# A mixture-of-experts block on one core: slot regions per expert, the router by halves, four shared units behind each loop

## The chip, the core and the metric

The kernel runs on one core of a Trainium2 chip, in one launch. TensorE (PE), VectorE (DVE), ScalarE (ACT), GpSimd (POOL) and SyncE (SP, which issues the direct DMAs) each run their own instruction stream and meet at semaphores. The metric is the device time of the launch in microseconds. Three runs of the kernel before gave 469.31, 472.06 and 475.77 us; the median is 472.06 us.

## The reference

The input is 1,024 tokens of 256 numbers. Three sublayers follow each other, each with a residual:

```
x = x + 0.5 * ffn(layernorm(x))
x = x + attention(layernorm(x))        # gated linear attention, 2 heads of 128, chunks
x = x + 0.5 * ffn(layernorm(x))        # the same weights as the first ffn

ffn(x):
    shared = (silu(x @ g) * (x @ u)) @ down * sigmoid(x @ sgate)      # width 704
    p = softmax(x @ gate_w.T)                                        # 16 experts
    w, ids = top_k(p, 4)
    for e in range(16):
        coef = sum(where(ids == e, w, 0))
        out += coef * ((silu(x @ w1[e]) * (x @ w3[e])) @ w2[e])       # width 176
    return shared + out
```

Every token goes through the shared expert and through the four experts with its largest probabilities.

## The kernel before, in words

A token tile is 128 tokens, so there are NT = 8. Each ffn (f = 0, 1) has these stages.

- **Norm and router.** DVE normalises the tiles into `XR` (`norm`, L979), PE turns them into `XT` and computes the logits (`logits`, L392). When all 8 are there, DVE picks the four experts of each token (`choose`, L1035), PE ranks the choices by expert (`ranks`, L399), and DVE turns rank plus the expert's first slot into a slot number per choice (`places`, L1066). An expert's slots follow those of the expert before it, rounded up to 128, so `places` needs the counts over all tokens. `tables` (L1084) then computes, for each of the TL = 47 slot tiles, its expert (`tab`) and which rows are real (`valid`).
- **Dispatch.** POOL writes each token's row (normalised values, its 16 coefficients, its number) to its four slots in `slots_dram`: 8 x 4 = 32 indirect DMAs of 128 rows (L881). All slots were filled with zeros at the start (L315, L316; 6.5 MB).
- **Front.** Beside that PE computes the shared expert in 12 units: 6 slices of its width (the last one half as wide) for each half of the tokens. `unit_in` (L406) computes gate and up, ACT the silu, DVE the product (`unit`, L989), `unit_out` (L424) the way back down. FRONT = 11 of the 12 units stand ahead of the slot loop, the last one behind it. ACT and DVE split the experts' weights into a high and a low part between the units (`part` and `part2`, by the tables PARTED and PARTED2); for f = 1 only the low parts are done anew.
- **Slot loop.** 47 tiles: SP loads tile i into one of 6 buffers (L349), PE turns it, multiplies it with the expert's weights, and so on; the expert's number is read from `tab` into a register. POOL adds the result to one of three sum tables in DRAM (L896).
- **Behind the loop.** SP reads the sum tables back (L358, L364), DVE and POOL add them to X (`combine`, `add_tables`), and the shared part of tiles 4 to 7 is added to X once all 12 units are done (L1157). PE then runs 40 warm-up matmuls (L566) and the attention's first turned tiles.

The order of the work is written out by hand in each engine's function. In `attention` PE, ACT and DVE step through the 8 tiles in a loop over i; for f = 1 the norm and the logits of tile t are done inside it (`turned(2, t)`, `logits(1, t)`, `stats(2, t)`, `scale(2, t)`).

## Time and profile before

| | |
|---|---|
| median of 3 runs | 472.06 us |
| the profiled execution | 475.44 us |
| its span | 473.6 us |
| granted TensorE clock, mean | 0.961 |
| PE busy | 420.9 us, 89% |
| DVE busy | 286.2 us, 60% |
| POOL busy | 254.7 us, 54% |
| ACT busy | 210.8 us, 45% |

The profiled execution is 1.8 us longer than its span. A busy share is an average over stages with different limits, so it says little of what a change in one stage is worth. The stages, read off the timeline, in us from the span's start: first norm and router to 31, first front to 92, first slot loop to 193, sums and their way back to 212, attention to 282, second router to 293, second front to 346, second slot loop to 448, end to 473.6.

### The profile page before, as it was taken

The page shows a single profiled execution, that of the slowest core. Times are in us where ns is not written, and L with a number is a line of the kernel's source. Part 1 is how long each engine was busy: PE and PEld are TensorE (multiplying, and loading weights), DVE is VectorE, ACT ScalarE, POOL GpSimd, SP SyncE. Part 2 cuts the span into 40 slices and gives each one's busy share as a digit, 9 for nine tenths or more (in the row PEclk, how much of TensorE's full clock was granted, in tenths as well). Part 3 has the DMA queues.
Part 4 walks back from the last instruction along what each step waited for, and adds up shares of the span by engine and source line. Part 5 has one row for each costly group of instructions (what it writes and reads, how often), then busy time and mean ns, then how long its engine had stood idle before and what let it go on. Part 6 is the DMA issues. An engine that isn't in the chain of part 4 may idle for free.

```text
span 473.6 us, 8663 instructions
## 1 busy us (share of the span) xinstructions
PE 420.9 (89%) x2281; PEld 322.6 (68%) x2281; DVE 286.2 (60%) x843; ACT 210.8 (45%) x580; POOL 254.7 (54%) x209
## 2 busy tenths in 40 slices
PE   5899996799999999879969988999999999999910
PEld 3646553588999998534549964555668999999710
DVE  6485746666666666226496648675456666666406
ACT  2314537556666666303745641111125666666500
POOL 6037773047777777555055201776707677777710
PEclk9999999899999999897998999999999999999965
DMA  7999997369998776770000039722257788777665
GB/s 261 409 357 388 244 365 273 125 144 191 195 173 137 128 135 90 142 237 34 1 1 0 2 122 379 287 72 96 96 185 117 129 138 133 134 133 126 70 172 204
DMA packets 50477, 78.39 MB, mean 166 GB/s; under 512 B 5664, under 2 KB 41504, under 8 KB 49568
## 3 DMA queue, kind: packets, MB, share of 16 engines
q1 hardware_dynamic: 33824, 56.47, 36.3%
q0 software_dynamic: 16608, 21.37, 28.1%
q8 instruction: 22, 0.36, 0.3%
q14 instruction: 23, 0.19, 0.1%
HBM read 41.69 MB, written 36.13 MB: 164 GB/s over the span
## 4 chain that ended last, share of the span: by engine, by line
PE 57%; DMA 11%; DVE 10%; POOL 9%; issue 7%; ACT 4%; SPq 0%; DVEq 0%; POOLq 0%; another core or an unknown queue 0%; ACTq 0%
POOL slots L881 7%; DMA sums<-ar,idx 6%; PE ps L468 6%; PE ps L464 5%; PE ps L465 5%; PE ps L449 4%; PE ps L437 4%; PE ps L476 3%; PE ps L551 3%; PE ps L415 3%; PE ps L420 3%; PE ps L494 2%; PE ps L389 2%; PE ps L382 2%; PE ps L496 2%
## 5 line engine op out<-in xcount | busy, mean ns | idle before, releaser
L896 POOL DMA_INDIRECT sums<-ar,idx x94 | 145.4, 1547 | 85.2 <-ACT ar L735 73.6
L881 POOL DMA_INDIRECT slots<-XR,pos x64 | 72.3, 1130 | 65.1 <-DVE pos L1082 43.0
L1108 DVE SCALAR_TENSOR_TENSOR ar<-ps,XR,ar 128x176 f32<-128x176 f32 x94 | 37.6, 400 | 63.6 <-ACT ar L720 58.9
L464 PE MATMUL ps<-WH,xt 128*128 x188 | 62.2, 332 | 1.9 <-ACT xt L715 1.9
L465 PE MATMUL ps<-WL,xt 128*128 x188 | 60.7, 323 | 0.0
L720 ACT ACTIVATE ar<-ps 128x176 f32<-128x176 f32 x94 | 29.8, 317 | 64.4 <-PE ps L468 51.8
L437 PE MATMUL ps<-WS,ar 128*128 128x256 f32 (+1 forms) x192 | 48.3, 397 | 10.5 <-DVE ar L995 6.3
L437 PEld LDWEIGHTS ps<-WS,ar 128*128 128x128 f32 (+1 forms) x192 | 37.0, 197 | 28.3 <-issue 16.7
L709 ACT ACTIVATE ar<-ps 128x512 f32<-128x512 f32 (+1 forms) x24 | 14.3, 595 | 80.6 <-PE ps L415 65.1
L415 PE MATMUL ps<-XT,WS 128*128 128x512 f32 x96 | 47.4, 617 | 0.0
L468 PE MATMUL ps<-WH,xl 128*128 x188 | 46.5, 328 | 0.5 <-DVE xl L1125 0.3
L1125 DVE TENSOR_TENSOR xl<-ps,xt 128x256 fp32r<-128x256 f32 x94 | 39.8, 424 | 8.4 <-issue 4.4
L735 ACT ACTIVATE ar<-ps 128x256 f32<-128x256 f32 x94 | 36.1, 384 | 17.0 <-PE ps L500 13.3
L715 ACT ACTIVATE xt<-ps 128x256 fp32r<-128x256 f32 x94 | 36.1, 384 | 12.0 <-PE ps L449 11.7
L1119 DVE TENSOR_TENSOR hl<-ps,ht 128x256 fp32r<-128x256 f32 x94 | 39.2, 417 | 1.4 <-ACT ht L725 1.4
L449 PE MATMUL ps<-cst,XR 128*128 128x128 f32 x188 | 37.4, 280 | 0.6 <-DMA XR<-slots 0.2
L420 PE MATMUL ps<-XT,WS 128*128 128x512 f32 x80 | 37.7, 593 | 0.0
L464 PEld LDWEIGHTS ps<-WH,xt 128*128 128x128 f32 x188 | 35.2, 187 | 3.2 <-issue 2.8
L476 PE MATMUL ps<-cst,ar 128*128 128x128 f32 x188 | 36.0, 273 | 0.9 <-DVE ar L1113 0.5
L725 ACT ACTIVATE ht<-ps 128x256 fp32r<-128x256 f32 x94 | 35.7, 380 | 1.0 <-PE ps L476 1.0
L995 DVE TENSOR_TENSOR ar<-ps,ar 128x512 f32<-128x512 f32 x20 | 13.8, 690 | 36.7 <-PE ps L420 16.2
L465 PEld LDWEIGHTS ps<-WL,xt 128*128 128x128 f32 x188 | 35.4, 188 | 0.1
(155 smaller groups left out, 835.7 us busy)
## 6 DMA issues: line engine op xcount, KB each, us to landing
XR<-slots SPq DMA_DIRECT2D x94, 138.0 KB
WR<-w SPq DMA_DIRECT2D x8, 1408.0 KB, 13.9
slots<-ar SPq DMA_DIRECT2D x1, 6072.0 KB, 22.4
W2R<-w2a SPq DMA_DIRECT2D x2, 2048.0 KB
WR<-sums SPq DMA_DIRECT2D x16, 256.0 KB, 5.2
sums<-zeros SPq DMA_DIRECT2D x20, 128.0 KB
sums<-ar SPq DMA_DIRECT2D x2, 1152.0 KB
sums<-X SPq DMA_DIRECT2D x2, 1024.0 KB, 5.1
```

What stands on the lines that cost most here:

```text
L415: mm = pe.matmul(ps[:, 4 + u % 2, :], WS1[:, k, 2 * j, :], XT[:, k, half(h)], start=k == 0, stop=k == KD - 1)
L420: mm = pe.matmul(ps[:, 6 + u % 2, :], WS1[:, k, 2 * j + 1, :], XT[:, k, half(h)], start=k == 0, stop=k == KD - 1)
L437: mm = pe.matmul(ps[:, 2 * h + i // 2, i % 2 * D:(i % 2 + 1) * D], Hs[u % 2][rows, tok(i)], WS2[rows, j, :], start=first and i % 2 == 0, s ...
L449: mm = pe.transpose(ps[:, i % 2, k * P:(k + 1) * P], xs[i % NX][:, k * P:(k + 1) * P], ident)
L464: pe.matmul(to, token, WH[:, bass.ds(e, 1), k, :].rearrange("p a n -> p (a n)"), start=k == 0, stop=False)
L465: pe.matmul(to, token, WL[:, bass.ds(e, 1), k, :].rearrange("p a n -> p (a n)"), start=False, stop=False)
L468: mm = pe.matmul(to, xl[i % 2][:, k * P:(k + 1) * P], WH[:, bass.ds(e, 1), k, :].rearrange("p a n -> p (a n)"), start=False, stop=k == KD - 1)
L476: mm = pe.transpose(ps[:, 6 + i % 2, c * P:(c + 1) * P], hm[i % 2][:, c * P:(c + 1) * P], ident)
L881: pool.indirect_dma_start(out=slots_dram[:, :], out_offset=bass.IndirectOffsetOnAxis(ap=pos[:, t, r:r + 1], axis=0), in_=XR[:, t, :], in_o ...
L896: pool.indirect_dma_start(out=sums_dram[f][a][:, :], out_offset=bass.IndirectOffsetOnAxis(ap=idx[:, i:i + 1], axis=0), in_=ys[i % NY], in_ ...
L1119: dve.tensor_tensor(hl[i % 2], ps[:, 6 + i % 2, 0:2 * P], ht[i % 2].bitcast(F32), ALU.subtract).then_inc(s_hl, 1)
L1125: dve.tensor_tensor(xl[i % 2], ps[:, i % 2, 0:D], xt[i % 2].bitcast(F32), ALU.subtract).then_inc(s_xl, 1)
```

## The change

Every expert gets a region of CAP = 1,152 rows of `slots_dram`, at a fixed start. A slot number is now the rank plus a constant, so it needs no counts of the later tokens. The router (`choose`, `ranks`, `places`, ACT's `router`) runs by halves of four tiles, and POOL's dispatch waits for one half at a time. For f = 0 half 0 is routed before the second half is normalised; for f = 1 it is routed inside the attention's loop, and half 1 behind it. The fill at the start shrinks to one tile; instead SP writes one tile of zeros behind the last token of each expert (16 DMAs, `tails`), at an address that it reads into a register. `counts` and `tables` also compute the first row of each slot tile, and SP reads it into a register before each of the 94 loads. FRONT goes from 11 to 8, so four units stand behind each loop; the tables PARTED and PARTED2 move with it. POOL signals by a memset behind its last add, and SP waits for that before it reads the sums back.

```diff
-PARTED = {3: (0, 3), 4: (3, 6), 5: (6, 9), 6: (9, 13), 7: (13, NE)}
+PARTED = {1: (0, 2), 2: (2, 6), 3: (6, 10), 4: (10, 14), 5: (14, NE)}
-PARTED2 = {8: (0, 8), 9: (8, NE)}
+PARTED2 = {5: (0, 4), 6: (4, 12), 7: (12, NE)}
-SLOTS = TL * P
+CAP = N + P
+SLOTS = NE * CAP + P
-FRONT = UNITS - 1
+FRONT = (8, 8)
+HT = NT // 2
...
-            fill = slots_dram.rearrange("(p t) n -> p (t n)", p=P)
-            most = TL // ZR * ZR * ROW
-            sp.dma_start(fill[:, 0:most].rearrange("p (t n) -> p t n", n=ZR * ROW), spread(blank, 1, TL // ZR)).then_inc(s_fill, 16)
-            sp.dma_start(fill[:, most:], blank[:, 0:TL % ZR * ROW]).then_inc(s_fill, 16)
+            sp.dma_start(slots_dram[NE * CAP:, :], zeros[:, :]).then_inc(s_fill, 16)
...
+            def row(of, i):
+                return nc.values_load(of[0:1, i:i + 1], engines=[mybir.EngineType.SP], min_val=0, max_val=NE * CAP,
...
+            def tails(f):
+                sp.wait_ge(s_last, f + 1)
+                for e in range(NE):
+                    sp.dma_start(slots_dram[bass.ds(row(last_row, e), P), :], zeros[:, :]).then_inc(s_fill, 16)
+            tails(0)
...
+                    tails(1)
+                sp.wait_ge(s_tab, f + 1)
+                sp.wait_ge(s_fill, 16 * (1 + NE * (f + 1)))
                 sp.wait_ge(s_disp, 16 * NT * TOPK * (f + 1))
                 for i in range(TL):
                     wait(sp, s_hm, TL * f + i - NX + 1)
-                    sp.dma_start(xs[i % NX], slots_dram[tok(i), :]).then_inc(s_xs[i % NX], 16)
+                    sp.dma_start(xs[i % NX], slots_dram[bass.ds(row(first_row, i), P), :]).then_inc(s_xs[i % NX], 16)
...
+                sp.wait_ge(s_added, f + 1)
...
+            def ranks(f, h):
+                pe.wait_ge(s_sel, 2 * f + h + 1)
+                if h == 1:
+                    count = ps[:, 3, RK + NT * NE:RK + NT * NE + NE]
+                    pe.matmul(count, ones[:, :], upto[0][:, :, HT - 1], start=True, stop=False)
+                    pe.matmul(count, ones[:, :], upto[1][:, :, HT - 1], start=False, stop=True)
+                to = ps[:, ranks_bank(f, h), RK + h * HT * NE:RK + (h + 1) * HT * NE]
+                pe.matmul(to, ones[:, :], upto[h][:, :, :].rearrange("p e t -> p t e"), start=True, stop=False)
+                if h == 1:
+                    pe.matmul(to, ones[:, :], spread(upto[0][:, :, HT - 1], 1, HT), start=False, stop=False)
+                pe.matmul(to, minus_later, gt[:, tiles_of(h), :].rearrange("p t e -> p (t e)"), start=False, stop=True).then_inc(s_rank, 1)
...
                 if u == NJ:
-                    pe.wait_ge(s_pos, f + 1)
-                if u == FRONT:
+                    pe.wait_ge(s_tab, f + 1)
+                if u == FRONT[f]:
...
-                    for t in range(NT + 1):
-                        if t < NT:
+                    for t in range(HT + 1):
+                        if t < HT:
                             turned(0, t)
                         if t > 0:
                             logits(0, t - 1)
-                unit_in(f, 0)
-                ranks(f)
-                unit_in(f, 1)
-                unit_out(f, 0)
-                for u in range(2, FRONT):
+                    unit_in(0, 0)
+                    ranks(0, 0)
+                    unit_in(0, 1)
+                    for t in range(HT, NT + 1):
+                        if t < NT:
+                            turned(0, t)
+                        if t > HT:
+                            logits(0, t - 1)
+                    unit_out(0, 0)
+                    unit_in(0, 2)
+                    ranks(0, 1)
+                else:
+                    pe.wait_ge(s_pos, 3)
+                    unit_in(1, 0)
+                    ranks(1, 1)
+                    pe.wait_ge(s_sgx, 4)
+                    unit_in(1, 1)
+                    unit_out(1, 0)
+                    unit_in(1, 2)
+                unit_out(f, 1)
+                for u in range(3, FRONT[f]):
...
+                    if i == NT + 3:
+                        ranks(1, 0)
...
+                    if c == 0 and 2 * q == HT:
+                        router(0, 0)
...
                     norm(0)
-                router(f)
-                for u in range(FRONT):
+                    unit(0, 0)
+                router(f, 1)
+                for u in range(1 - f, FRONT[f]):
                     unit(f, u)
                     if f == 0:
                         part(u)
                         part2(u)
                 slots(f)
-                for u in range(FRONT, UNITS):
+                for u in range(FRONT[f], UNITS):
...
+                    if i == NT + 1:
+                        router(1, 0)
...
-                pool.wait_ge(s_fill, 32)
-                pool.wait_ge(s_pos, f + 1)
                 for t in range(NT):
+                    pool.wait_ge(s_pos, 2 * f + t // HT + 1)
...
+                pool.memset(mark[:, :], 0.0).then_inc(s_added, 1)
...
+            def choose(f, h):
+                some = tiles_of(h)
+                dve.wait_ge(s_lg, 2 * f + h + 1)
...
+            def places(f, h):
+                some = tiles_of(h)
+                dve.wait_ge(s_rank, 2 * f + h + 1)
+                rank = ps[:, ranks_bank(f, h), RK + h * HT * NE:RK + (h + 1) * HT * NE].rearrange("p (t e) -> p t e", e=NE)
+                link(dve.tensor_tensor(lg[:, some, :], rank, spread(base1, 1, HT), ALU.add))
+                link(dve.tensor_tensor(ex[:, some, :], lg[:, some, :], gt[:, some, :], ALU.mult))
+                for t in range(HT * h, HT * (h + 1)):
+                    ins = dve.max(m8[:, t, :], ex[:, t, :])
+                link(ins)
+                dve.tensor_scalar(pos[:, some, :], m8[:, some, 0:TOPK], -1.0, None, ALU.add).then_inc(s_pos, 1)
+            def counts(f):
+                dve.wait_ge(s_rank, 2 * f + 2)
+                count = ps[:, 3, RK + NT * NE:RK + NT * NE + NE]
+                dve.scalar_tensor_tensor(last_row[:, :], count, -1.0, base1, ALU.add, ALU.add).then_inc(s_last, 1)
                 link(dve.tensor_scalar(ti[:, :], count, float(P - 1), None, ALU.add))
                 link(dve.tensor_scalar(ti[:, :], ti[:, :], 7, None, ALU.logical_shift_right))
                 link(dve.tensor_copy(tf[:, :], ti[:, :]))
                 link(dve.tensor_tensor_scan(cum[:, :], ones[:, 0:NE], tf[:, :], 0.0, ALU.mult, ALU.add))
                 link(dve.tensor_tensor(low[:, :], cum[:, :], tf[:, :], ALU.subtract))
                 link(dve.tensor_scalar(low[:, :], low[:, :], float(P), None, ALU.mult))
...
                 dve.tensor_tensor(high[:, :], low[:, :], count, ALU.add)
-                dve.tensor_scalar(pos[:, :, :], m8[:, :, 0:TOPK], -1.0, None, ALU.add).then_inc(s_pos, 1)
+                link(dve.tensor_scalar(tf[:, :], tf[:, :], float(-P), float(CAP), ALU.mult, ALU.add))
...
+                link(dve.tensor_tensor(cmp[:, :, :], cmp[:, :, :], spread(tf[:, :], 1, TL), ALU.mult))
+                link(dve.tensor_reduce(v2[:, :], cmp[:, :, :], AX.X, ALU.add))
+                link(dve.scalar_tensor_tensor(v2[:, :], tile_no, float(P), v2[:, :], ALU.mult, ALU.add))
+                dve.tensor_scalar(first_row[:, :], v2[:, :], float(NE * CAP), None, ALU.min)
...
             def ffn(f):
-                choose(f)
-                places(f)
-                unit(f, 0)
-                unit(f, 1)
+                if f == 0:
+                    unit(0, 0)
+                    choose(0, 1)
+                    unit(0, 1)
+                    places(0, 1)
+                else:
+                    choose(1, 1)
+                    places(1, 1)
+                    unit(1, 0)
+                    unit(1, 1)
+                counts(f)
                 tables(f)
-                for u in range(2, NJ + 1):
-                    unit(f, u)
-                    part(f, u)
-                shared_sums(f, 0, NJ)
-                for u in range(NJ + 1, FRONT):
+                part(f, 1)
+                for u in range(2, FRONT[f]):
                     unit(f, u)
                     part(f, u)
                     part2(f, u)
-                shared_sums(f, 1, FRONT)
+                    if u == NJ:
+                        shared_sums(f, 0, NJ)
+                shared_sums(f, 1, FRONT[f])
                 slots(f)
-                for u in range(FRONT, UNITS):
-                    unit(f, u)
+                if f == 0:
+                    for u in range(FRONT[f], UNITS):
+                        unit(f, u)
...
+                    if i == NT + 1:
+                        choose(1, 0)
+                    if i == NT + 2:
+                        places(1, 0)
...
-            norm(0, lambda t: None)
...
+            norm(0, range(HT), lambda t: None)
...
+            choose(0, 0)
+            places(0, 0)
+            norm(0, range(HT, NT), lambda t: None)
             ffn(0)
-            norm(1, lambda t: combine(0, t))
+            norm(1, range(NT), lambda t: combine(0, t))
             attention()
             ffn(1)
             for t in range(NT):
+                if t < 2:
+                    unit(1, FRONT[1] + 2 * t)
+                    unit(1, FRONT[1] + 2 * t + 1)
                 combine(1, t)
```

Three places where instructions move, in the words of the built programs. First, DVE in the first norm. Before, the last two tiles are scaled and the whole router follows:

```order
L971 BN_STATS st<-X 128x6 [waits s_x3]
L972 BN_AGGR mv<-st 128x2 [waits s_chain]
L977 TENSOR_SCALAR XR<-X,mv,rstd 128x256 [waits s_mv,s_rs] x2
L1179 COPY XR<-ics 128x8 [waits s_ics]
L1038 TENSOR_REDUCE t<-ps 128x8 [waits s_lg,s_cst]
L1039 TENSOR_TENSOR lg<-ps,t 128x128 [waits s_chain]
L1041 TENSOR_REDUCE t<-ex 128x8 [waits s_ex]
L1042 RECIPROCAL t<-t 128x8 [waits s_chain]
```

In the changed kernel the same four statistics stand behind the first half's slot numbers (`pos`), and the first unit's product (L1065) stands ahead of the second half's `choose`:

```order
L1146 TENSOR_SCALAR pos<-m 128x16 [waits s_chain]
L1041 BN_STATS st<-X 128x6 [waits s_x2]
L1042 BN_AGGR mv<-st 128x2 [waits s_chain]
L1041 BN_STATS st<-X 128x6 [waits s_x2]
L1042 BN_AGGR mv<-st 128x2 [waits s_chain]
L1041 BN_STATS st<-X 128x6 [waits s_x3]
L1042 BN_AGGR mv<-st 128x2 [waits s_chain]
L1047 TENSOR_SCALAR XR<-X,mv,rstd 128x256 [waits s_mv,s_rs] x2
L1041 BN_STATS st<-X 128x6 [waits s_x3]
L1042 BN_AGGR mv<-st 128x2 [waits s_chain]
L1047 TENSOR_SCALAR XR<-X,mv,rstd 128x256 [waits s_mv,s_rs] x2
L1065 TENSOR_TENSOR ar<-ps,ar 128x512 [waits s_uu,s_usi]
```

So `choose` and `places` of half 0 moved ahead of the statistics of tiles 4 to 7, and the product of unit 0 ahead of `choose` of half 1.

Second, DVE at the end of the attention. Before, the last token tiles are added to X (L1236), their statistics taken and scaled, and the router (L1038) follows:

```order
L1236 SCALAR_TENSOR_TENSOR X<-ps,rr,X 128x256 [waits f_r]
L971 BN_STATS st<-X 128x6 [waits s_xu]
L972 BN_AGGR mv<-st 128x2 [waits s_chain]
L977 TENSOR_SCALAR XR<-X,mv,rstd 128x256 [waits s_mv,s_rs]
L1236 SCALAR_TENSOR_TENSOR X<-ps,rr,X 128x256 [waits f_r]
L971 BN_STATS st<-X 128x6 [waits s_xu]
L972 BN_AGGR mv<-st 128x2 [waits s_chain]
L977 TENSOR_SCALAR XR<-X,mv,rstd 128x256 [waits s_mv,s_rs] x2
L1038 TENSOR_REDUCE t<-ps 128x8 [waits s_lg]
```

In the changed kernel `choose` of half 0 stands ahead of the last of these adds (L1327), and its `places` (L1141 to L1146) ahead of the last scale. The rows begin with the last two of `choose`:

```order
L1134 TENSOR_SCALAR t<-sgt 128x4 [waits s_sgx]
L1135 RECIPROCAL gate<-t 128x4 [waits s_chain]
L1327 SCALAR_TENSOR_TENSOR X<-ps,rr,X 128x256 [waits f_r,s_chain]
L1041 BN_STATS st<-X 128x6 [waits s_xu]
L1042 BN_AGGR mv<-st 128x2 [waits s_chain]
L1047 TENSOR_SCALAR XR<-X,mv,rstd 128x256 [waits s_mv,s_rs]
L1141 TENSOR_TENSOR lg<-ps,cst 128x64 [waits s_rank]
L1142 TENSOR_TENSOR ex<-lg,gt 128x64 [waits s_chain]
L1144 MAX m<-ex 128x8 [waits s_chain]
L1144 MAX m<-ex 128x8 x3
L1146 TENSOR_SCALAR pos<-m 128x16 [waits s_chain]
L1047 TENSOR_SCALAR XR<-X,mv,rstd 128x256 [waits s_mv,s_rs]
```

The last tile's add, statistics and scale now stand behind the whole of `choose`, and the scale behind `places` too.

Third, PE behind the first slot loop: the units, the 40 warm-up matmuls and the first turned tile. Before:

```order
L498 MATMUL ps<-W2H,hl 128x256 [waits s_hl]
L500 MATMUL ps<-W2B,hl 128x256
L415 MATMUL ps<-XT,WS 128x512 [waits s_uh]
L415 MATMUL ps<-XT,WS 128x512
L437 MATMUL ps<-WS,ar 128x256 [waits s_uh,s_y]
L437 MATMUL ps<-WS,ar 128x256 x3
L382 MATMUL ps<-warm 128x512 x40
L389 MATMUL ps<-cst,XR 128x128 [waits s_xc,s_xn]
```

In the changed kernel three more units stand there; the rows show the last part of them:

```order
L459 MATMUL ps<-XT,WS 128x512
L464 MATMUL ps<-XT,WS 128x512 x2
L481 MATMUL ps<-WS,ar 128x256 [waits s_uh]
L481 MATMUL ps<-WS,ar 128x256 x3
L459 MATMUL ps<-XT,WS 128x512 [waits s_uh]
L459 MATMUL ps<-XT,WS 128x512
L481 MATMUL ps<-WS,ar 128x256 [waits s_uh]
L481 MATMUL ps<-WS,ar 128x256 x3
L481 MATMUL ps<-WS,ar 128x256 [waits s_uh]
L481 MATMUL ps<-WS,ar 128x256 x3
L419 MATMUL ps<-warm 128x512 x40
L426 MATMUL ps<-cst,XR 128x128 [waits s_xc,s_xn]
```

The 40 warm-up matmuls and the turned tile behind them stand behind all four units.

## Rows read from the trace of the kernel before

**Rows 1.** Page, the chain that ended last, shares by line.
```profile
POOL slots L881 7%; DMA sums<-ar,idx 6%; PE ps L468 6%; PE ps L464 5%; PE ps L465 5%; PE ps L449 4%; PE ps L437 4%; PE ps L476 3%; PE ps L551 3%; PE ps L415 3%; PE ps L420 3%; PE ps L494 2%; PE ps L389 2%; PE ps L382 2%; PE ps L496 2%
```

**Rows 2.** Table by window, first slot loop: busy time by engine, clock, DMA.
```profile
92.00:194.00 102.00, 99.91 (x707) 91.72 (x706) 64.73 (x236) 60.86 (x187) 69.68 (x45) 1.00 0.80 150
```

**Rows 3.** Chain of waits, first front: start us, us, what.
```profile
32.78 1.72 PE ps L415 x4
...
36.21 1.73 PE ps L437 x8
```

**Rows 4.** Timeline, end of the first front: start us, us, engine, line.
```profile
42.07 2.48 DVE L1007 TENSOR_TENSOR WL<-WR,WH 128x704 fp32r<-128x704 f32 x3
...
69.94 0.60 ACT L709 ACTIVATE ar<-ps 128x512 f32<-128x512 f32 x1 [4.50 <-PE ps L415]
...
85.46 3.57 PE L437 MATMUL ps<-WS,ar 128*128 128x256 f32 x8 [4.28 <-DVE ar L995]
...
91.96 0.36 DVE L1125 TENSOR_TENSOR xl<-ps,xt 128x256 fp32r<-128x256 f32 x1
```

**Rows 5.** Timeline, both dispatches on POOL, and SP behind them.
```profile
30.98 1.14 POOL L881 DMA_INDIRECT slots<-XR,pos  x1 [23.18 <-DVE pos L1082]
...
74.99 1.13 POOL L881 DMA_INDIRECT slots<-XR,pos  x1 [0.30 <-issue]
...
80.77 2.71 SPq L349 DMA_DIRECT2D XR<-slots  x6
...
293.10 1.03 POOL L881 DMA_INDIRECT slots<-XR,pos  x1 [19.84 <-DVE pos L1082]
...
340.37 1.96 POOL L881 DMA_INDIRECT slots<-XR,pos  x1 [0.30 <-issue]
...
343.83 2.71 SPq L349 DMA_DIRECT2D XR<-slots  x6
```

**Rows 6.** Timeline, PE behind the first slot loop.
```profile
193.40 1.88 PE L415 MATMUL ps<-XT,WS 128*128 128x512 f32 x4
...
199.35 9.76 PE L382 MATMUL ps<-warm 128*128 128x512 bf16 x40
212.10 1.42 PE L389 MATMUL ps<-cst,XR 128*128 128x128 f32 x4 [2.99 <-DVE XR L977]
```

**Rows 7.** Timeline, end of attention and second router: PE, then DVE.
```profile
277.03 0.52 PE L395 MATMUL ps<-WG,XT 128*128 128x17 f32 x4
...
278.03 0.48 DVE L1236 SCALAR_TENSOR_TENSOR X<-ps,rr,X 128x256 f32<-128x256 f32 x1 [1.71 <-ACT rr L836]
...
282.63 0.29 DVE L1038 TENSOR_REDUCE t<-ps 128x8 f32<-128x128 f32 x1 [2.42 <-PE ps L395]
...
288.43 0.20 DVE L1064 RECIPROCAL gate<-t 128x8 f32<-128x8 f32 x1
...
290.62 0.29 DVE L1076 TENSOR_TENSOR lg<-ps,low 128x128 f32<-128x128 f32 x1
...
293.48 0.18 DVE L1090 COPY idx<-ics 128x47 int32<-128x47 int32 x1
...
299.64 0.21 DVE L1095 TENSOR_TENSOR valid<-v 128x47 int32<-128x47 f32 x1
```

**Rows 8.** Timeline, behind the second slot loop: PE, then DVE.
```profile
447.93 1.88 PE L415 MATMUL ps<-XT,WS 128*128 128x512 f32 x4
...
461.93 1.68 DVE L1152 TENSOR_TENSOR X<-X,WR 128x256 f32<-128x256 f32 x4 [10.77 <-DMA WR<-sums]
...
471.01 0.48 DVE L1026 SCALAR_TENSOR_TENSOR X<-ps,gate,X 128x256 f32<-128x256 f32 x1
```

**Rows 9.** Chain of waits, a table load of ACT and what follows.
```profile
233.87 1.28 ACT L799
235.17 0.64 ACT ar L803
```

**Rows 10.** Chain of waits, a register read of DVE.
```profile
94.20 0.52 DVEq L1099
```

147 lines of the change are left out of this document (74 added, 73 removed).

## The prediction

> **What bounds the kernel now.** I read the page first: no engine bounds the whole, and the dispatch has the largest single share of the chain of waits, 7% [rows 1]. So the time is a sum of stages, and I read each from the timeline.
>
> In the first slot loop PE is busy 99.9 of 102 us at full clock [rows 2]. The change alters nothing in that loop but SP's loads, so the loops (2.17 us a tile, 47 tiles, twice) are kept. What counts is when each loop starts and what follows it.
>
> - First front: the first dispatch goes out at 30.98 and the last at 74.99, SP loads the first slot tile at 80.77 [rows 5], but DVE begins the loop at 91.96 [rows 4]. The dispatch is not the limit there: ACT and DVE are still splitting weights, and PE waits 4.28 us for them [rows 4].
> - Second front: dispatch from 293.10, last one at 340.37, slot load at 343.83 [rows 5]. Here the dispatch is the limit, since the weights' high parts are already there.
> - Behind the first loop: PE ends the loop at 193.40, has one half unit and 40 warm-up matmuls, waits 2.99 us and turns the first tile at 212.10 [rows 6]. The sums' way through DRAM is the limit, by 3 us only.
> - Behind the second loop: from 447.93 to DVE's last add at 471.01 (ends 471.49); DVE waited 10.77 us for the sums until 461.93 [rows 8].
>
> **Prices.** On PE one unit is `gate`, `up` and `out`, 1.72 us each by the chain's spacing: 1.72 (L415) and 1.73 (L437) [rows 3], the L420 group as L415. That is 5.16 us, and 3.45 for a half-wide unit. A whole `choose` on DVE lasts from 282.63 to 288.63, 6.0 us, `places` from 290.62 to about 292.3, 1.7 us, `tables` from 293.48 to 299.85, 6.4 us [rows 7]. With half the width these are chains of short dependent operations, so they do not halve: I take 4.6 and 1.2 us (bounds: half and whole, 3.0 to 6.0 and 0.8 to 1.7). A low part of one expert is 0.83 us (2.48 for three) [rows 4].
>
> **Term 1, the first front.** The times here are estimates, walked operation by operation with the prices above. Half 0 has its slot numbers at about 21.7: its four logits are ready at about 13.5, `choose` takes 4.1 until its scan, PE is inside unit 0 until about 19.3, then ranks and `places`. POOL starts at 22.3 rather than 30.98. Its 32 DMAs take 45 us as before, since half 1's slot numbers come at 39.5, long before POOL has done 16. The slot loads could start at 22.3 + 45.1 + 4.7 (from the last DMA's end to the load, before) = 72.
>
> DVE and ACT are later. The second half's statistics now follow `places` on DVE, unit 0 ends at about 31.5, `choose` and `places` of half 1 at 39.5. ACT loads its table for silu, for exp, and for silu again, two loads more than before. A load takes 1.28 us and the next operation starts 0.02 us after it [rows 9], so I price them at 2.6 us, half of it hidden while DVE ends its product: 1.3 us, in the 39.5. Then `counts` (new, nine short operations, 1.9 us), `tables` with two more passes of 0.94 and two short ones (8.7 us), low parts of two experts (1.7 us): unit 2's product on DVE ends at 52.4. PE has had only one more `unit_in` in the meantime and stands from 43.4 to 52.4. From there PE paces units 3 to 5: silu of unit 5 at 61, and 1 us later because after 9 us without work it starts at the lower clock, as the 8 matmuls behind the 4.28 us wait show (3.57 us instead of 1.73) [rows 4]. From silu of the third last unit before the loop to the loop itself it was 91.96 - 69.94 = 22.0 us [rows 4]. The same work follows silu 5, with two more high parts (1.4 us) and 1 us of waits for DVE between them: 62 + 24.4 = 86.4. The gain is 91.96 - 86.4 = **5.5 us**. Bounds: 14 us if only the dispatch limited it, -1 us if PE's wait spreads.
>
> The 6.5 MB fill that is gone and the 2.2 MB of tails cost nothing here: the tails' addresses are ready at 40, 16 of them at 0.97 us (0.52 us for a register read [rows 10] and 0.45 for an issue, 2.71 us for six [rows 5]) end at 56, far before 72. If a tail took 2.0 us they would still end at 72.
>
> On the table load: the trace has 1.31 us from its start to the next operation. The Trainium skill (ScalarE: Activation LUTs, What ACT_TABLE_LOAD costs) states about 2.66 us for a switch, a drain of 1.38 us included. By that the two loads would cost 2.8 us more and term 1 would be about 3 us; the trace decides, and it shows no drain.
>
> **Term 2, behind the first loop.** PE has units 8 to 11: 3 x 5.16 + 3.45 = 18.9 us, then 40 warm-up matmuls, 9.76 before [rows 6], 8.7 at full clock. The first tile is turned 27.7 us behind the loop's end instead of 212.10 - 193.40 = 18.7: 9.0 us later. The 3 us limit by the sums is gone, nothing else takes its place: DVE's product of unit 11 ends 17 us behind the loop, its statistics follow by 19. Some comes back, since PE no longer waits ahead of the turned tiles: the first two took 1.42 us for four matmuls [rows 6], twice what they take at full clock, and 8 warm-up matmuls behind them ran as slowly; at full clock the ten-odd matmuls save 1.7 us. I take **+7.3 us**. Bounds: +5 (DVE and ACT also catch up) and +10.
>
> **Term 3, end of attention and second front.** The logits of tile 3 end at 277.5, DVE's add of tile 7 started at 278.03 [rows 7]. Now `choose` of half 0 stands between: 277.6 to 282.2, so that add, and with it the last tile, the weights' reload and half 1's logits, are 4.2 us later. `places` of half 0 adds 1.3 to the last scale. Half 0's slot numbers come at 285.0, POOL starts at 285.9 instead of 293.10: **7.2 us earlier**. Half 1's come at 294, before POOL has done 16 DMAs at 306. Dispatch takes 50.7 us from its first DMA to the slot load, as before [rows 5], so the load is at 336.6, and 0.5 us later for the register read before it [rows 10]. PE has 8 units from 287: 38 us, a stand of 4 us at `tables`, then 18 warm-up matmuls: about 336.5. DVE ends its last sums at 336.2. Dispatch, PE and DVE meet within 1 us. I take **-6.7 us** (bounds -8 and -2, the second if PE or DVE is late by 5).
>
> **Term 4, the end.** PE's four units end 19.1 us behind the loop. DVE waits for the sums until 14.0 us behind it, as before (461.93) [rows 8], then it has two products of about 0.7 us between the adds, and unit 11's cannot end before 17.1. From there 3 tiles of 0.84 (1.68 for two) and 4 of 1.38 (0.48 more for the shared part, and a gap) end at 25.2 us [rows 8]; before it was 471.49 - 447.93 = 23.6. **+1.6 us** (bounds +0.5 and +4). POOL's memset and SP's wait for it delay the first readback by 1.7 us; it hides beside the last add's landing, and costs at most those 1.7.
>
> **Sum.** -5.5 + 7.3 - 6.7 + 1.6 = -3.3 us. The profiled execution of before took 475.44 us, so its like would take 472.1. That execution is among the slowest of the runs shown, 3.4 us above the median; taken from the median, 472.06 - 3.3 = **468.8 us**.
>
> **Rivals.**
>
> *The units behind the loops are free and the first front comes down to its dispatch.* For it: DVE waits 10.77 us behind the second loop [rows 8], and the dispatch would allow a load at 72. Against it: the 40 warm-up matmuls stay behind the units on PE. Price: term 1 up to -14, term 2 at +5, term 3 at -7, term 4 at +1: -15, or 457 us; with the bounds only half reached, -11. About 459 us. Chance 0.22.
>
> *SP's register reads slow the slot loop; this ends slower.* The place is SP's queue in the loop: each load now waits for a read of `first_row`, and the next read starts only when the load is issued. With 0.45 us for the issue and 2.17 us a tile it decides from a read of 1.7 us, in the first loop's 19 tiles with a zeroing DMA from 1.3. At 2.2 us it would cost 0.48 x 94 + 0.43 x 19 = 53 us, 522 us. Against it: DVE reads such a register in every tile, 0.52 us at the longest seen [rows 10]. The Trainium skill (DMA: Bandwidth & Descriptors, Latency and other measured facts) has a floor of about 600 ns for such a read, which would not decide either. Chance 0.05.
>
> *The halves buy nothing*: term 1 is eaten by PE's and DVE's stands, and the second dispatch grows because the weights' reload (7.6 MB) and the tails now run beside it. The second dispatch took 49.2 us for 32 DMAs [rows 5], 1.54 each; at 1.7 the second front gains 1.6 us only. Sum 0 + 7.3 - 1.6 + 1.6 = +7: 479 us. Chance 0.13, a third of it above 2%.
>
> **How the numbers follow.** The forecast has 0.60, within 461 to 477. From the rivals the range takes the first down to 458 and leaves the other tails out: 458 to 478. Two per cent, about what a measurement can tell from no change here, is 9.4 us: faster means below 462.6. The first rival lies mostly there (0.18), and the forecast's low end adds 0.04; slower is the second rival, a third of the third and a little of the forecast, 0.10. Same: 0.68.
>
> **What would show it.** First POOL dispatch near 22 and 286; DVE's first `xl` of the loop near 86; PE idle some 9 us while DVE runs `tables` in the first front; the first turned tile 28 us behind the first loop; SP's slot loads at their old spacing; DVE's last add 25 us behind the second loop. The forecast is wrong if PE does not stand in the first front, or if the loop takes more than 2.2 us a tile.

## The result, and the profile after

The changed kernel took 483.06 us (median of 4 runs, 481.72 to 483.61), the kernel before 471.14 us beside it (469.31 to 475.77). The ratio is 1.023, with a 95% interval of 1.015 to 1.031. I had forecast 468.8 us, 458 to 478: both the direction and the range were wrong.

The profiled executions are 482.55 us after and 475.44 us before, so the profiles have 7.1 us of the difference. Both are cut at the same points. "Left" is VectorE's first `xl` of a slot loop, "keys" the first matmul of `keys_in`.

| stretch, us | before | after | my term | measured |
|---|---|---|---|---|
| start to first left | 91.96 | 91.15 | -5.5 | -0.8 |
| first loop | 101.4 | 103.1 | 0 | +1.7 |
| loop to keys | 24.95 | 31.25 | +7.3 | +6.3 |
| keys to second left | 128.5 | 127.5 | -6.7 | -1.1 |
| second loop | 101.0 | 100.7 | 0 | -0.3 |
| end | 23.6 | 24.9 | +1.6 | +1.3 |

Both losses are about as large as I had said. The two gains are missing. The changed kernel's page shows that the dispatch, 7% of the chain before [rows 1], has left it, and that 2% are waits whose end it puts down to "another core or an unknown queue" ("remote" in the other views):

```profile
PE 76%; DVE 12%; ACT 5%; issue 4%; another core or an unknown queue 2%; DMA 1%; DVEq 0%; ACTq 0%
```

**First front.** This is the timeline around the second half's ranks (start, duration, engine, line, and in brackets the idle time before and what ended it):

```profile
33.94 0.69 DVE L1065 TENSOR_TENSOR ar<-ps,ar 128x512 f32<-128x512 f32 x1
...
37.94 0.35 PE L448 MATMUL ps<-gt,cst 128*128 128x64 f32 x2
...
40.96 0.96 POOL L949 DMA_INDIRECT slots<-XR,pos  x1 [0.30 <-issue]
41.62 1.88 PE L464 MATMUL ps<-XT,WS 128*128 128x512 f32 x4
44.48 0.23 DVE L1141 TENSOR_TENSOR lg<-ps,cst 128x64 f32<-128x64 f32 x1 [9.85 <-remote]
44.63 0.60 ACT L775 ACTIVATE ar<-ps 128x512 f32<-128x512 f32 x1 [5.78 <-remote]
...
45.89 0.96 POOL L949 DMA_INDIRECT slots<-XR,pos  x1 [3.97 <-DVE pos L1146]
```

The first store is early as forecast (21.74, before 30.98 [rows 5]). But VectorE, which waits for the ranks of L448, does not go on at 38.3, when they end. It goes on at 44.48, 9.85 us idle, and ScalarE's wait for TensorE ends 0.15 us later. The releaser is "remote": the view finds no instruction that ended just before. The event itself is in the trace, among the recorded semaphore updates. TensorE's update for the ranks stands there at 44.46, and its next three, for matmuls that end at 40.07, 41.78 and 43.50 by the timeline, at 44.55, 44.61 and 44.67. So it is TensorE's updates that are late, in a bunch; VectorE and ScalarE go on 0.02 us behind theirs. `places`, the counts and the tables all come 6 us later than the matmuls would allow, and VectorE then works with few gaps to 91.15.

The profile of the kernel before has such late updates too, in its first front, and I had overlooked them: ScalarE waits there for a `gate` that ends at 58.97 and whose update is recorded at 62.78. In e19 below, the same program up to its warm-ups ahead of the loop, each update of TensorE's in that stretch comes within 0.02 us. The first row is of before, the second of e19:

```profile
62.81 0.60 ACT L709 ACTIVATE ar<-ps 128x512 f32<-128x512 f32 x1 [5.25 <-remote]
```
```profile
59.02 0.60 ACT L709 ACTIVATE ar<-ps 128x512 f32<-128x512 f32 x1 [2.24 <-PE ps L415]
```

Its first left comes at 87.18, with 18 warm-ups more ahead of it, against 91.96. So the 91.96 that I took for the front of before holds some 5 us of these late updates, and the -0.8 is measured from there.

**Behind the first loop.** TensorE (compare [rows 6]):

```profile
194.25 1.88 PE L459 MATMUL ps<-XT,WS 128*128 128x512 f32 x4
...
213.47 8.81 PE L419 MATMUL ps<-warm 128*128 128x512 bf16 x40
222.11 0.60 PE L426 MATMUL ps<-cst,XR 128*128 128x128 f32 x4
...
225.50 1.10 PE L613 MATMUL ps<-XT,WR 128*128 128x512 f32 x2 [0.62 <-ACT XT L750]
```

The first turned tile is 27.9 us behind the loop; I had 27.7. No idle time stands before it: the 40 warm-ups do, while VectorE had the tile ready at about 213.5.

**Second front.** TensorE, then GpSimd, SyncE and VectorE (compare [rows 5, 7]):

```profile
296.33 1.44 PE L419 MATMUL ps<-warm 128*128 128x512 bf16 x3
...
297.56 3.37 PE L459 MATMUL ps<-XT,WS 128*128 128x512 f32 x4
```
```profile
292.62 1.03 POOL L949 DMA_INDIRECT slots<-XR,pos  x1 [12.22 <-DVE pos L1146]
...
313.69 0.97 POOL L949 DMA_INDIRECT slots<-XR,pos  x1 [5.99 <-DMA slots<-XR,pos]
```
```profile
346.48 4.46 SPq L385 DMA_DIRECT2D XR<-slots  x6
348.21 4.05 PE L419 MATMUL ps<-warm 128*128 128x512 bf16 x18
...
352.99 0.42 DVE L1209 TENSOR_TENSOR xl<-ps,xt 128x256 fp32r<-128x256 f32 x1 [1.17 <-issue]
```

The attention was 7.1 us later, so the first store at 292.62 is, counted from `keys_in`, 7.6 us earlier, as forecast (7.2). From it to the slot load 53.9 us pass, not 50.7. TensorE leaves the attention at the lower clock (granted 0.50 from 292 to 300; three warm-ups 1.44 us, four `gate` matmuls 3.37 instead of 1.88), ends its units at 348.2, and has 18 warm-ups left before it may turn the first slot tile.

### The profile page after: what moved, and what is told of

Same layout as the page of the kernel before. It is cut to its first block, busy times and chain, and to the rows that moved or that the text cites. A ratio compares the mean times of both kernels' runs of the same rounds, so it can differ in the third digit from the quotient of the medians.

```text
span 480.7 us, 9177 instructions
## 1 busy us (share of the span) xinstructions
PE 427.9 (89%) x2297; PEld 328.8 (68%) x2297; DVE 295.6 (61%) x895; ACT 214.2 (45%) x586; POOL 252.0 (52%) x211
## 4 chain that ended last, share of the span: by engine, by line
PE 76%; DVE 12%; ACT 5%; issue 4%; another core or an unknown queue 2%; DMA 1%; DVEq 0%; ACTq 0%
PE ps L459 8%; PE ps L512 7%; PE ps L481 7%; PE ps L508 7%; PE ps L509 6%; PE ps L464 6%; PE ps L493 5%; PE ps L520 4%; PE ps L419 4%; PE ps L613 3%; PE ps L538 3%; PE ps L540 2%; PE ps L539 2%; PE ps L542 2%; PE ps L544 2%
## 5 line engine op out<-in xcount | busy, mean ns | idle before, releaser
L949 POOL DMA_INDIRECT slots<-XR,pos x64 | 69.4, 1085 | 56.1 <-DVE pos L1146 30.1
L481 PE MATMUL ps<-WS,ar 128*128 128x256 f32 (+1 forms) x192 | 51.3, 416 | 22.3 <-DVE ar L1065 15.1
L481 PEld LDWEIGHTS ps<-WS,ar 128*128 128x128 f32 (+1 forms) x192 | 38.8, 207 | 38.7 <-issue 16.7
L786 ACT ACTIVATE ar<-ps 128x176 f32<-128x176 f32 x94 | 29.9, 318 | 67.2 <-PE ps L512 38.3
L459 PE MATMUL ps<-XT,WS 128*128 128x512 f32 x96 | 50.1, 648 | 0.0
L464 PE MATMUL ps<-XT,WS 128*128 128x512 f32 x80 | 37.6, 592 | 0.0
L512 PEld LDWEIGHTS ps<-WH,xl 128*128 128x128 f32 x188 | 31.2, 191 | 5.3 <-DVE xl L1209 4.4
```

The source lines that it names most:

```text
L459: mm = pe.matmul(ps[:, 4 + u % 2, :], WS1[:, k, 2 * j, :], XT[:, k, half(h)], start=k == 0, stop=k == KD - 1)
L464: mm = pe.matmul(ps[:, 6 + u % 2, :], WS1[:, k, 2 * j + 1, :], XT[:, k, half(h)], start=k == 0, stop=k == KD - 1)
L481: mm = pe.matmul(ps[:, 2 * h + i // 2, i % 2 * D:(i % 2 + 1) * D], Hs[u % 2][rows, tok(i)], WS2[rows, j, :], start=first and i % 2 == 0, s ...
L512: mm = pe.matmul(to, xl[i % 2][:, k * P:(k + 1) * P], WH[:, bass.ds(e, 1), k, :].rearrange("p a n -> p (a n)"), start=False, stop=k == KD - 1)
L949: pool.indirect_dma_start(out=slots_dram[:, :], out_offset=bass.IndirectOffsetOnAxis(ap=pos[:, t, r:r + 1], axis=0), in_=XR[:, t, :], in_o ...
```

## The experiments

Every kernel ran beside the kernel before on the same chip; ratios are to that, with 95% intervals. The stretches are from each one's profile, cut as above.

**One half of the change each.** e1 has the halves and regions, with eleven units ahead of each loop:

```diff
-FRONT = (8, 8)
+FRONT = (11, 11)
```

> The changed kernel with eleven units ahead of each loop again (and the splitting of the weights spread as before): regions and halves alone. Theory (the four units behind each loop cost 6.3 and 1.3 us there and each front is bound by TensorE and VectorE, no longer by the dispatches): three more units of 5.7 us lengthen each front by about 17 us, the stretches behind the loops fall by 7.6, so 483 + 34 - 7.6, about 509 us; first slot's subtraction near 108 us. Rival (units are free in a front that waits for dispatches): 483 - 7.6 = 475 us, first slot's subtraction near 91.

Measured: 499.1 us, ratio 1.052 [1.044, 1.061]; first left 104.2, loop to keys 23.0, keys to second left 142.6. So the units are not free ahead of the loops: three of them cost 13.0 and 15.1 us there, and what moving them gives back is 8.2 us behind the first loop and 3.9 at the end. The direction of the first theory holds, its size was 10 us too large.

e2 is the kernel before with `FRONT = 8` and the change's `PARTED` tables.

> The kernel before with only the units moved: eight ahead of each loop, four behind. Theory: the first front falls from 91.96 to the end of its dispatches and the slot load after them (80.77 plus 2 to 3, so 83 to 84), the second stays at its dispatches (0), behind the loops +6.3 and +1.3: 471 - 8.5 + 7.6, about 470 us. Rival (the front is held by splitting the weights on VectorE, which the units covered): 471 + 7.6 = 479 us with the first slot's subtraction still past 90.

Measured: 480.8 us, 1.013 [1.004, 1.022], 11 us above the first theory. First left 84.9 (-7.1), loop to keys 31.24 (+6.3) and end +1.3 are as expected within 1.5. But the second front was 5.0 longer, which no theory had, and the loops 1.8 and 1.1. Part of the 5.0 is the clock: the warm-ups between the last tiles of the attention ran at the lower one (granted 0.50 from 280 to 286), and the logits came 2.9 us later behind the last sum than before. TensorE:

```profile
280.01 1.44 PE L382 MATMUL ps<-warm 128*128 128x512 bf16 x3
...
351.63 0.69 PE L449 MATMUL ps<-cst,XR 128*128 128x128 f32 x2 [16.19 <-DMA XR<-slots]
```

The second line is TensorE's wait for the first slot tile: 16.2 us, so with eight units a second front of whole stores is bound by its stores. No update of TensorE's that ended a wait is late in it.

**Term 2: the warm-ups.**

```diff
-                keep_warm(40, 4)
+                keep_warm(4, 4)
```

> The changed kernel with 4 instead of 40 warm-up matmuls between the units behind the first loop and the attention's first turned tile. Theory (the four units took the place of the warm-ups, and both now stand in a row ahead of that tile): the tile comes 5 to 8 us sooner, 475 to 478 us in all. Rival (the tile waits for the adds of the sums or VectorE's norms anyway): the same 483 us, TensorE idle in place of the warm-ups; or the clock falls without them and the projections lose what is won.

Measured: 476.1 us, 1.009 [1.005, 1.013]. Loop to keys falls from 31.25 to 24.1, less than the 24.95 of before. TensorE:

```profile
213.72 1.04 PE L419 MATMUL ps<-warm 128*128 128x512 bf16 x4
214.59 0.60 PE L426 MATMUL ps<-cst,XR 128*128 128x128 f32 x4
```

So term 2 was these warm-ups, which the units had made needless.

**Term 1: what VectorE waits for.** e4 loads half of `WR`, `W2Q` and `W2R` only behind the counts:

```diff
             for e in range(0, NE, 4):
+                if e == 8:
+                    sp.wait_ge(s_last, 1)
```

> The changed kernel with the last half of the experts' first weights and all of their second weights loaded only once the counts of the first router are there (about 41 to 46 us). Theory (VectorE's 9.85 us ahead of the second half's places are an instruction fetch that stands behind weight loads in full DMA queues): that wait falls to the 4.3 us in which TensorE's ranks come, the counts and tables 5 us sooner, 478 us in all. Rival (it is the dispatches' traffic, or something apart from the loads): the wait stays at 9 us or more, and 483 us.

Measured: 484.3 us, 1.021 [1.014, 1.028], VectorE's wait 9.88 us. The table by window (busy of PE, PEld, DVE, ACT, POOL; clock; DMA share; GB/s), of the changed kernel and of e4, shows that the queues were much less busy in e4 (DMA share 0.34 against 0.96):

```profile
35.00:40.00 5.00, 5.00 (x25) 3.60 (x24) 0.00 (x0) 3.31 (x5) 3.78 (x5) 1.00 0.96 197
```
```profile
35.00:40.00 5.00, 5.00 (x23) 3.41 (x23) 0.00 (x0) 3.31 (x5) 3.78 (x5) 1.00 0.34 113
```

My first explanation, full queues of weight loads, is refuted. e5 holds the stores in its place:

```diff
-                    pool.wait_ge(s_pos, 2 * f + t // HT + 1)
+                    pool.wait_ge(s_pos, 2 * f + (t // HT + 1 if f == 1 else 2))
```

> The changed kernel with the first front's stores to the slots held until both halves have their places (about 39 to 46 us) in place of starting at 21.7. Theory A (the stores' traffic or GpSimd's work is what keeps VectorE and ScalarE waiting to 44.5 us): the wait ahead of the second half's places falls from 9.9 to the 4 us in which TensorE's ranks come, places near 39. Theory B (something in VectorE's own instruction stream at that point): the wait stays at 9.9. Either way the stores then run to about 39 + 41 = 80 (A) or 46 + 41 = 87 us (B), and the first slot is held to 84 to 91; 480 to 485 us.

VectorE, and at the end the same engine at the loop:

```profile
39.39 0.23 DVE L1141 TENSOR_TENSOR lg<-ps,cst 128x64 f32<-128x64 f32 x1 [4.16 <-PE ps L448]
...
93.38 0.42 DVE L1209 TENSOR_TENSOR xl<-ps,xt 128x256 fp32r<-128x256 f32 x1 [7.33 <-ACT xt L781]
```

The wait is 4.16 us and ends with the ranks: theory A, and e6, e7 and e8 on the same chip have it at 9.8 to 9.9. Its second front, where the stores run as in the changed kernel, still has late updates (1.45 and 4.6 us). Without the 7.33 us for late stores VectorE would have been ready at 86.0; I had forecast 86.4. The time is 484.2 us, 1.024 [1.016, 1.033], since the stores now end at 87.8.

e6 puts 64 one-column memsets ahead of VectorE's first norm.

> The changed kernel with 64 memsets of one column ahead of VectorE's first norm (0 to 2 us of work), so that each later instruction of VectorE stands 64 places further in its stream. Theory B (VectorE waits at a place of its instruction stream, such as the edge of a fetched block): the 9.9 us wait ahead of the second half's places moves to another instruction or goes, ScalarE's of 5.8 us stays; if it lands where VectorE waits anyway, 478 us. Rival (the wait belongs to the data: ranks, stores): it stays at that line with 9 to 10 us, and 483 to 485 us.

Measured: 482.8 us, 1.023 [1.014, 1.032]; the wait stayed at its line with 9.87 us. It is not a place in VectorE's instruction stream. The Trainium skill (Runtime: NRT & Kernel Launch, Instruction fetch mechanics) has fetched blocks of 256 instructions, of which one more 16 KB block is read while the last is executed. The changed kernel's page agrees on the size (queue q8, instruction: 22 packets, 0.36 MB). An edge of such a block would have moved by 64. That TensorE's own stream is at fault, whose updates are the late ones, was not tested.

e9 issues 8 stores early and the rest behind the second half's places; e17, the same with 12:

```diff
-                    pool.wait_ge(s_pos, 2 * f + t // HT + 1)
+                    pool.wait_ge(s_pos, 2 * f + (1 if t < 2 else 2))
```

> The changed kernel with a pause in the stores: the first 8 go out as soon as the first half has its places, the other 24 once the second half has. In the first front 8 stores are issued by 32 us, 2 us before VectorE begins to wait for TensorE's ranks. Theory (stores in flight hold that wait to 22.7 us after the first of them): the wait falls to 4.2 us, places near 39.4, first slot's subtraction at 86 to 87 as the prediction had it; in the second front 1 to 2 us more: 476 us. Rival (any early store starts the same 22.7 us): wait stays 9.9, 483 us.

> The changed kernel with the pause behind 12 early stores instead of 8, so that stores are issued until 37 us, across the begin of VectorE's wait at 34.6. Theory (the wait lasts while stores issued ahead of it are under way, and ends with them): it ends 2 to 3 us after the last of the 12, at 39 to 40 us, 1 us past the ranks. Rival (a fixed 22.7 us after the first store): 44.5 us as in the changed kernel.

e9: 481.0 us, 1.012 [1.005, 1.018]; VectorE:

```profile
39.25 0.23 DVE L1141 TENSOR_TENSOR lg<-ps,cst 128x64 f32<-128x64 f32 x1 [4.05 <-PE ps L448]
...
85.78 0.36 DVE L1209 TENSOR_TENSOR xl<-ps,xt 128x256 fp32r<-128x256 f32 x1
```

e17: 475.4 us, 1.008 [1.003, 1.013]; wait 3.58 us, first left 85.6. The first front is now as long as forecast (86.4). Of the 5.4 us that it gains on the changed kernel e9 keeps only 2 in the median: its second front is 1.9 longer than the changed kernel's and its second loop 2.2, where TensorE stood 4.48 us for the first slot tile. e17's second front is 1.9 shorter. A wait of fixed length behind the first store (22.7 us in the changed kernel) is not seen in either.

e12 waits for each of the first 16 stores before the next.

> The changed kernel with each of the first half's 16 stores waited for by GpSimd before it issues the next (in the first front), so that at most one is in flight while VectorE waits for the ranks. Theory C (the number in flight holds the wait): it falls to 4.2 us. Theory D (GpSimd's issuing of stores alone does): it stays 6 us or more beyond the ranks. The first half's stores end later (16 of 3 to 4 us, to 70 to 85 us), so the first front is then bound by them: 485 to 495 us, and only the wait is read.

Measured: 511.7 us, 1.079 [1.070, 1.087]; the wait is 3.77 us and ends with the ranks, although stores were under way. That would be theory C, but its second front, in which nothing was changed, has lost its late updates as well.

Another rival stands beside e9, e12 and e17, and no run tests it: the chip. e1 to e4 ran on one, e5 to e8 on a second, and there each kernel with halves has late updates in one front or both. e9 to e19 ran on three others, and in none of their ten profiles does a late one end a wait, in either front. The changed kernel itself has no profile there. So only e5, among its like on the same chip, shows that holding the stores ends the wait in the first front; that a pause or spacing does is not shown.

**Term 3: the second front.** e7 moves `tables` behind unit 3, e8 has `keep_warm(6, B_KV)` instead of 3 a step and 8 ahead of the first unit.

> The changed kernel with the 10 us of tables on VectorE moved behind the unit with number 3, in both fronts. Theory (in the first front VectorE is busy from 44.5 to 91 us and its sum stays, in the second TensorE stands 5.0 us for it and is then at the lower clock): first slot's subtraction unchanged in the first front (within 1 us), 4 to 6 us sooner in the second, 478 us. Rival (TensorE's stand is only moved behind the tables): the same 483 us.

> The changed kernel with more warm-up matmuls at the attention's end (6 instead of 3 a step and 8 ahead of the second front's first unit). Theory (TensorE comes out of the attention at the lower clock: the unit's first four matmuls take 3.37 us instead of 1.88): they take 1.9 us, the ranks of the second half come 1.5 to 3 us sooner, 480 to 481 us. Rival (the chain waits for ScalarE and VectorE there, or the extra matmuls delay logits): 483 us or above.

e7: 482.9 us, 1.022 [1.014, 1.030]; first left 90.6, second front 128.2. The rival holds. In the first front TensorE's stand of 14.6 us became two, of 6.1 and 4.8; in the second its stand of 5.0 us was only moved (5.98, up to 332.55), and nothing was gained. e8: 483.0 us, 1.024 [1.015, 1.032]. The four `gate` matmuls take 1.88 us, as the theory had it, and the ranks' matmuls end 1.2 us sooner (302.5). But their update came at 305.2, 2.7 us late; VectorE's wait grew from 4.29 to 5.71 us and ended at 305.3, in the changed kernel at 305.4.

Then I added up what had worked. e10 is e9 with 4 warm-ups behind the first loop, e11 also has 4 instead of 18 ahead of the second loop.

> The kernel of the stores with a pause, and 4 warm-ups in place of 40 behind the first loop. The two savings lie in different stretches and should add: 483 - 5 to 7 - 7, 469 to 471 us, no slower than the kernel before. Rival: the pause saves nothing, 476 us.

> As the one with the pause and 4 warm-ups behind the first loop, and 4 in place of 18 ahead of the second loop, where TensorE's units now end at 348 and the slot load is issued at 346.5: those 18 (4.05 us) no longer stand in the shadow of the stores. Theory: 2 to 3 us less, 466 to 468 us. Rival (the first slot load has not landed sooner, or the loop starts at the lower clock): no difference to that kernel.

e10: 474.7 us, 1.003 [1.000, 1.007], 4 us above its theory. e11: 472.8 us, 0.998 [0.994, 1.002]; the 18 warm-ups were worth 1.8 us. In e11 the order at the loop has changed: TensorE

```profile
327.52 3.62 PE L481 MATMUL ps<-WS,ar 128*128 128x256 f32 x16
330.98 1.03 PE L419 MATMUL ps<-warm 128*128 128x512 bf16 x4
338.34 0.69 PE L493 MATMUL ps<-cst,XR 128*128 128x128 f32 x2 [6.34 <-DMA XR<-slots]
```

is through by 332 and waits 6.34 us for the stores. GpSimd had stood 7.49 us for the landing of its first twelve. e13 takes these stops out:

```diff
-                    if f == 1 and t in (2, 5):
-
-                        pool.wait_ge(s_disp, 16 * TOPK * (NT * f + t + 1))
```

> As e11 (pause, fewer warm-ups), without GpSimd's two waits for the landing of its stores in the second front (behind tiles 2 and 5), of which the first took 7.5 us. Theory (the second front is now bound by its stores, and the stop is what holds them: TensorE waited 6.3 us for the first slot load): last store 8 to 10 us sooner, first slot's subtraction 4 to 6 us sooner (TensorE's units end then), 467 to 469 us. Rival (the stores land no sooner, since the reload of the weights holds the queues): the slot load waits for their landing instead, 472 to 473 us.

Measured: 466.8 us, 0.988 [0.976, 0.999]. The last store starts at 327.5 (e11: 333.0), though the first started 1.3 later; second front 123.2. TensorE finds its tile ready:

```profile
332.33 1.03 PE L419 MATMUL ps<-warm 128*128 128x512 bf16 x4
333.19 0.38 PE L493 MATMUL ps<-cst,XR 128*128 128x128 f32 x2
```

e14 is e11 with VectorE's `choose(1, 0)` behind the last `added` and `stats`.

> As e11, with the last residual sum of the attention ahead of the first half's choice on VectorE and not behind it: the reload of the weights then starts about 4.5 us sooner and the first store about 4 us later. Theory (the reload's lateness behind the choice is what meets the stores, 289.8 against 278.5 before): the stop falls by 3 to 5 us, the end by 0 to 3 us, 470 to 473 us. Rival (what the stores lose at their start is not given back): 474 to 476 us.

Measured: 473.6 us, 0.999 [0.994, 1.004]. The reload started 3.2 us sooner (272.4), the first store 1.8 later, the stop was still 7.33 us. So the reload's start isn't what made the stop long.

**The first loop's 1.7 us.** e16 is e13 with `keep_warm((24, 4)[f], 6)`, e13 had 6 ahead of the first loop.

> As the one without stops, with 24 warm-ups in place of 6 ahead of the first loop, where TensorE stands 1.3 and 2.5 us and the loop's first matmuls then run at 0.49 instead of 0.32 us. Theory (the loop's 1.7 us more than before come from its start at the lower clock): loop 1.5 us shorter, 1 to 1.5 us less than without. Rival (VectorE's subtraction, not the clock, sets the start, or the loop's length has another cause): the same time.

Measured: **463.8 us, 0.980 [0.970, 0.990]**. The first loop takes 101.8 us (e13 103.1). The loop's second tile on TensorE, in e13 and in e16:

```profile
87.43 0.66 PE L508 MATMUL ps<-WH,xt 128*128 x1 [0.56 <-ACT xt L781]
```
```profile
88.24 0.42 PE L508 MATMUL ps<-WH,xt 128*128 x1 [0.56 <-ACT xt L781]
```

The clock is shown: from 79 to 92 us the granted clock is 0.78 in e13 and 1.00 in e16. The 18 warm-ups more cost 1.0 us ahead of the loop (first left 86.4 for 85.4) and save 1.3 in it, so hardly anything is left of them. The second front is 2.3 us shorter (121.0 for 123.2), which I had not expected. It is the clock at the end of the attention, where the edit changes nothing: the first `gate` matmuls of the second front, in e13 and in e16,

```profile
284.70 3.36 PE L459 MATMUL ps<-XT,WS 128*128 128x512 f32 x4
```
```profile
283.13 1.88 PE L459 MATMUL ps<-XT,WS 128*128 128x512 f32 x4
```

with a granted clock of 0.52 and 0.92 from 281 to 288. The second loop took 1.3 us more (101.3 for 100.0). By the profiles e16 is 1.3 us faster than e13, by the medians of four runs each 3.0, and e13's runs reach from 464.7 to 469.9.

**Two controls.**

> The fastest kernel so far (e16: pause, fewer warm-ups behind the first and ahead of the second loop, no stops, 24 warm-ups ahead of the first loop) with the pause behind 12 stores in place of 8. Theory (in e17 the wait stayed short with 12, and the stores that follow the pause end 5 us sooner in the second front): 461 to 463 us. Rival (TensorE's units and VectorE bound both fronts already): 463 to 464 us.

> The kernel before with the two edits of e16 that its program has too: no stops in the second front's stores, and 24 and 4 warm-ups ahead of the loops instead of 6 and 18. It tells what of the gain over before is the change's. Theory (its second front is held by eleven units on TensorE, which end at 341.7 us, 5 before the first slot's subtraction): 3 to 4 us less, 467 to 469 us, so the changed program's remainder is 4 to 5 us. Rival (the stops did all): 463 to 465 us. Other rival: no gain, 471 us.

e18 (e16, pause at 12): 464.9 us, 0.989 [0.980, 0.998], no better than e16: nearer its rival. e19 (before, without the stops, 24 and 4 warm-ups): 472.1 us, 1.001 [0.996, 1.005]. In its profile the second left is at 344.2, with TensorE's eleven units ending at 340.8. Its first front is the one shown above, without late updates. The two edits alone give the kernel before nothing that can be measured: the gain of e16, 2% (1 to 3), needs the change. The cut of the 40 warm-ups was not tried on the kernel before; they end there 2.99 us ahead of the tile that TensorE waits for [rows 6].

## Why the prediction was wrong

- **Term 1, -5.5 us, measured -0.8: wrong.** The step that failed is "choose and places of half 1 at 39.5": places began at 44.5 and ended at 45.6, since TensorE's update for the ranks came 6.2 us behind them. My walk had no such wait. Its prices held (the half `choose` takes 4.5 to 4.8 us, and each table load lasts 1.28 us with its activation 0.01 behind it). As for the drain of 1.38 us that the Trainium skill (ScalarE: Activation LUTs, What ACT_TABLE_LOAD costs) adds, the three loads of the changed kernel show none (26.63 + 1.28, next 27.92). Without late updates e9 has places ended at 40.4 (my 39.5) and the first left at 85.8 (my 86.4). A second step failed beside it, the 91.96 that I subtracted from: "ACT and DVE are still splitting weights, and PE waits 4.28 us for them" was a front with late updates. Against e19's 87.18 the walk, had it come true, would have gained 1 us and not 5.5 (with 18 warm-ups more ahead of e19's loop).
- **Term 2, +7.3, measured +6.3: right.** I had seen the 40 warm-ups stand behind the units. e3 shows that this was all of it: 24.1 without them, 24.95 before.
- **Term 3, -6.7, measured -1.1: wrong.** The step that failed is "dispatch, PE and DVE meet within 1 us", a sum of three ends with no margin. The store start was right (-7.6), but the dispatch took 53.9 instead of 50.7 us, TensorE came out of the attention at the lower clock and 3.4 us late, and 18 warm-ups stood behind it. I had named the 18 and not asked what hides them. That clock is not fixed by the code: e5 and e7, with the same attention, have 1.88 us for the `gate` matmuls that took 3.37. With stops and most warm-ups gone the stretch is 5.3 (e13) and 7.6 us (e16) shorter than before: such a kernel can give what I had said.
- **Term 4, +1.6, measured +1.3: right.**
- **The loops at 0** left out 1.7 us in the first, of which a start at full clock gives back 1.3 (e16).
- **The rivals.** The first front did not fall to its dispatch limit. Register reads are no hindrance: second loop 100.7 us for 101.0 before, with SyncE's loads in it 0.33 us each and its reads 0.28. (The 0.52 us "at the longest seen" was the longest on the chain; the longest of VectorE's 94 in the trace of before took 0.89.) "The halves buy nothing" is what happened (479 forecast, +7 of my sum and +7.1 in the profiles). I gave it 0.13; it deserved more, since the second gain rested on three engines ending together. That its +7 met the profiles is partly luck: it knew nothing of late updates, which lengthen both of them.
- **The median** moved 11.9 us and the profiles 7.1. The profiled execution of before is 4.3 above its median, and its first front is 4.8 above e19's. So the late updates are probably what makes it slow. To take term 1 from that front and the sum from the median counts them twice.

Open: why TensorE's updates come late. Shown is that VectorE's wait stood at 9.8 to 9.9 us in the changed kernel, e1, e3, e4, e6, e7 and e8, where 16 stores run on to 42 us, that less busy DMA queues (e4) and 64 more instructions of VectorE's (e6) leave it there, and that it is gone when the stores are held (e5). It does not need the change: the profile of before has late updates up to 78 us, about as long as its stores run (76.1), and that of e19, with the same stores, has none. With a pause or spaced stores (e9, e12, e17) it is gone too, but on chips where no profile has it.

## What to carry to other kernels

When work moves to a place where a filler kept an engine warm or hid a wait, cut the filler in the same edit, and look at every other filler and stop that was sized for the old bound: here they cost 7 us (e3), 2 (e11) and 6 (e13). A stage whose engines end within 1 us of each other has no gain to give until each of them is shortened. Before a stretch of one profile becomes the base of a forecast, look through it for waits that no instruction ended, and compare a second execution: here 5 us of the base were such waits. And look at the waits of the other engines while many small indirect stores run.

## What the runs showed of the hardware

- TensorE's semaphore updates can come late and in a bunch. In the changed kernel four are recorded from 44.46 to 44.67, for matmuls that end from 38.28 to 43.50, while GpSimd issued indirect stores every 1.27 us. DMA share 0.96 or 0.34 (e4) made no difference. In e9 to e17 the updates for the ranks come 0.01 or 0.02 us behind them. The same program can have it or not: in the first front 3.8 us in before, none in e19.
- GpSimd's wait for the landing of its first 12 stores of the second front took 6.0 us in the changed kernel and 7.5 in e11, with the reload of the weights issued 2.8 us ahead of the first store, and 1.75 in before, where it was issued 14.6 us ahead. But in e14, with 7.8 us between them, it was 7.3. Without the stops the stores ended 5.5 us sooner (e11, e13).
- In e12 one indirect store issued and waited for took 6.7 us (21.79 to 28.45) and the next one 14.2 (to 42.62), beside the weight loads, and the last seven of the sixteen 2.7 to 3.4 each, against 1.27 us where they follow each other.
- After the same code TensorE left the attention at either clock: granted 0.50 in the changed kernel (four `gate` matmuls 3.37 us), 1.88 us for them in e5 and e7.
